# Block-diagonal queries and values of a windowed attention: filled by SBUF-to-SBUF transfers instead of ScalarE and GpSimd, with the block number as innermost axis

## The reference

```python
x = x + _L0_xattn_ref(_layernorm(x, axis=-1), ctx_4096, ctx_4096)   # autocorrelation, top 9 shifts
x = x + _L0_ffn_ref(_layernorm(x, axis=-1), ...)                    # base matrix + 8 experts of rank 16
x = x + _L1_xattn_ref(_layernorm(x, axis=-1), ctx_4096, Wq, bq, ...) # the windowed attention
x = x + _L1_ffn_ref(_layernorm(x, axis=-1), ...)                    # 4 experts of rank 16

def _L1_xattn_ref(x, cond, Wq, bq, Wk, bk, Wv, bv, Wo, bo):
    B, C, T = x.shape                     # 32, 128, 1024
    H, W = (HEADS, WINDOW)                # 8, 16
    hd = C // H                           # 16
    q = _pointwise(Wq, bq, x)
    k = _pointwise(Wk, bk, cond)
    v = _pointwise(Wv, bv, cond)
    ...
    dots = jnp.einsum('bhdt,bhdtw->bhtw', qh, k_win) * scale
    attn = jax.nn.softmax(dots, axis=-1)
    out = jnp.einsum('bhtw,bhdtw->bhdt', attn, v_win)
    out = out.reshape(B, C, T)
    return _pointwise(Wo, bo, out)
```

## Time and profile before

| | |
|---|---|
| Time, median of 3 executions | 1869.83 us (1869.39 to 1873.03) |
| Profiled execution, span | 1871.1 us; this lies inside the spread of the three |
| Busy, share of the span | PE 92%, DVE 84%, ACT 73%, POOL 55% |
| TensorE clock granted | full (1.00) from 400 to 1400 us |
| Transfers | 77.82 MB, mean 42 GB/s |

### The profile page before, as it was taken

One profiled execution on the slowest core, in us unless ns is written; L12 is line 12 of the kernel. 1 busy time (PEld: TensorE's weight loads), 2 busy tenths in 40 slices (PEclk: granted clock), 3 DMA queues, 4 the chain that ended last, 5 costly groups with the idle time before them and its releaser, 6 DMA issues. The chain is left out here.

```text
span 1871.1 us, 48299 instructions
## 1 busy us (share of the span) xinstructions
PE 1712.3 (92%) x19296; PEld 1078.5 (58%) x19296; DVE 1575.8 (84%) x4726; ACT 1372.6 (73%) x2121; POOL 1028.3 (55%) x934
## 2 busy tenths in 40 slices
PE   3689999999999999999999999999999999999875
PEld 1355566666556656556666655666665566565543
DVE  5778898888888888889888888988888888888853
ACT  4277777878777787877777887778787777878753
POOL 1555556556555656655556655555565556566542
PEclk7899999999999999999999999999999999999995
DMA  5111110111010111101011110101110101111000
GB/s 208 34 35 36 35 46 25 47 46 46 24 47 27 44 46 47 47 24 47 24 47 46 47 38 33 46 25 47 46 46 24 47 28 43 46 47 35 2 12 24
DMA packets 20977, 77.82 MB, mean 42 GB/s; under 512 B 2704, under 2 KB 2960, under 8 KB 20240
## 3 DMA queue, kind: packets, MB, share of 16 engines
q1 hardware_dynamic: 20752, 74.72, 11.7%
HBM read 57.94 MB, written 16.78 MB: 40 GB/s over the span
## 5 line engine op out<-in xcount | busy, mean ns | idle before, releaser
L586 PE MATMUL pb<-w_base_h,even_words 128*128 128x512 f16 x1024 | 324.8, 379 | 0.0
L1438 POOL TENSOR_TENSOR p_hl<-sc,p_hl 128x512 f16<-128x512 f32 x128 | 164.2, 1283 | 206.6 <-ACT p_hl L764 206.6
L877 ACT ACTIVATE q_diag<-sc,par 32x512 f32<-32x512 f32 x384 | 269.4, 717 | 8.0
L1483 POOL TENSOR_TENSOR sc<-sc,sc_rec 128x512 f32<-128x512 f32 x128 | 134.4, 1050 | 216.8 <-DVE sc_rec L1245 216.6
L586 PE MATMUL pb<-w_base_l,even_words 128*128 128x512 f16 x512 | 193.9, 379 | 0.0
L473 PE MATMUL pa<-xn_a,tab 128*128 128x512 f32 x384 | 180.5, 606 | 4.6 <-ACT xn_a L764 4.6
L660 PEld LDWEIGHTS pc<-sc_t,v_diag 128*128 128x128 f16 x6144 | 170.2, 97 | 20.6 <-DVE sc_t L1252 6.0
L660 PE MATMUL pc<-sc_t,v_diag 128*128 128x32 f16 x6144 | 173.9, 177 | 5.6 <-DVE sc_t L1252 5.6
L637 PE MATMUL pc<-k_h,q_diag 128*128 128x32 f16 x2048 | 169.1, 177 | 0.0
L638 PE MATMUL pc<-k_l,q_diag 128*128 128x32 f16 x2048 | 168.4, 177 | 0.0
L639 PE MATMUL pc<-k_h,q_diag 128*128 128x32 f16 x2048 | 168.4, 177 | 0.0
(11 more groups left out here) (170 smaller groups left out, 5008.1 us busy)
## 6 DMA issues: line engine op xcount, KB each, us to landing
x_a<-in_x SPq DMA_DIRECT2D x32, 512.0 KB, 3.6
x_res<-in_ctx_in SPq DMA_DIRECT2D x32, 512.0 KB, 4.4
x_res<-in_x SPq DMA_DIRECT2D x32, 512.0 KB, 4.5
out<-rows_c SPq DMA_DIRECT2D x32, 512.0 KB, 2.9
v_diag<-in_base_w SPq DMA_DIRECT2D x4, 1024.0 KB, 10.4
q_diag<-in_ra SPq DMA_DIRECT2D x1, 544.0 KB, 14.1
q_diag<-in_b SPq DMA_DIRECT2D x1, 512.0 KB, 15.8
q_diag<-in_b SPq DMA_DIRECT2D x2, 256.0 KB, 17.0
```

The lines of the kernel that those rows point to most:

```text
L586: mm(pb[:, h, :], rows[:, cols], weights[:, j, h * HALF:(h + 1) * HALF], start=(j == 0 and m == 0), stop=False)
L877: nc.scalar.activation(q_diag[rows, blocks, col:col + QB], source, ACT.Copy, scale=par[rows, a:a + 1]).then_inc(qd_out.sem, 1)
L1438: g_.tensor_tensor(part[:, :, :, LO], sc[:, g % 2, :, :], part[:, :, :, HI], ALU.subtract)\
L1483: g_.tensor_tensor(sc[:, g % 2, :, :], sc[:, g % 2, :, :], sc_rec[:, blocks].unsqueeze(2).to_broadcast([P, GB, KEYS]), ALU.mult)\
```

## The change

Both buffers get the block number as innermost axis: `q_diag` is [rows, 128 columns, 64 blocks] and `v_diag` is [rows, odd/even, 128 columns, 32 blocks]. `q_hl` and `v_t` get the same order, so that what a head contributes is one contiguous run in a row. The copies of ACT and POOL go away. SP issues 8 transfers from `v_t` to `v_diag` (32 rows, two runs of 2 KB a row) and 8 from `q_hl` to `q_diag` (16 rows, a run of 4 KB a row) for each batch. The other four transfers are ordered anew in SP's loop. The first score group now waits for all queries of the batch.

```diff
-        q_diag = sb("q_diag", [P, NBLK, P])
-        v_diag = sb("v_diag", [P, NBLK, 2, P // 2])
+        q_diag = sb("q_diag", [P, P, NBLK])
+        v_diag = sb("v_diag", [P, 2, P, NBLK // 2])
...
+        q_words = q_hl.bitcast(F16).rearrange("p (t n two) -> p n t two", t=QB, two=2)
...
+            def place_values(b, odd):
+                sp.wait_ge(vt_out.sem, vt_out.after(b, odd + 1))
+                if odd == 0:
+                    sp.wait_ge(vdiag_set.sem, 1)
+                    if not first(b):
+                        sp.wait_ge(mm_av.sem, mm_av.after(b - 1))
+                for pair in range(PAIRS):
+                    rows = slice(32 * pair, 32 * pair + 32)
+                    place = v_diag[rows, odd, :, :].rearrange("p (a r d) m -> p a r (d m)", a=2, r=PAIRS)
+                    sp.dma_start(place[:, :, pair, :], v_t[odd][rows, :].rearrange("p (a n) -> p a n", a=2))\
+                        .then_inc(v_placed.sem, 16)
+
+            def place_queries(b):
+                sp.wait_ge(ql_out.sem, ql_out.after(b))
+                sp.wait_ge(qdiag_set.sem, 1)
+                if not first(b):
+                    sp.wait_ge(mm_sc.sem, mm_sc.after(b - 1))
+                for head in range(HEADS):
+                    rows = slice(HD * head, HD * (head + 1))
+                    sp.dma_start(q_diag[rows, rows, :], q_hl[rows, :].rearrange("p (t n) -> p t n", t=QB))\
+                        .then_inc(q_placed.sem, 16)
...
                 if live(1):
                     load_x_res(i - 1)
-                if live(3):
-                    store(i - 3)
+                if live(2):
+                    place_values(i - 2, 0)
+                if live(-1) and not first(i):
+                    load_x(i + 1)
+                if live(2):
+                    place_values(i - 2, 1)
+                    place_queries(i - 2)
                 if live(-1):
                     load_ctx(i + 1)
-                if live(-2):
-                    load_x(i + 2)
+                if live(3):
+                    store(i - 3)
...
-                if g % 2 == 0:
-                    pe.wait_ge(qd_out.sem, qd_out.after(b, (g // 2 + 1) * 2 * (PAIRS - 1)))
-                    pe.wait_ge(qd_pool.sem, qd_pool.after(b, (g // 2 + 1) * 2))
                 if g == 0:
+                    pe.wait_ge(q_placed.sem, q_placed.after(b))
...
-                    mm(place, q_halves[:, blk, :, HI], k_h[:, keys], start=False, stop=False)
-                    mm(place, q_halves[:, blk, :, HI], k_l[:, keys], start=False, stop=False)
-                    last = mm(place, q_halves[:, blk, :, LO], k_h[:, keys], start=False, stop=(i == GB - 1))
+                    mm(place, q_halves[:, :, blk, HI], k_h[:, keys], start=False, stop=False)
+                    mm(place, q_halves[:, :, blk, HI], k_l[:, keys], start=False, stop=False)
+                    last = mm(place, q_halves[:, :, blk, LO], k_h[:, keys], start=False, stop=(i == GB - 1))
...
-                        last = mm(place, v_halves[:, blk, :, v_part], p_halves[:, g % 2, i, :, p_part],
+                        last = mm(place, v_halves[:, blk % 2, :, blk // 2, v_part], p_halves[:, g % 2, i, :, p_part],
...
-                nc.scalar.activation(words(q_hl)[:, :, HI], pb_all, ACT.Identity, bias=bias_att[:, 0:1])\
+                nc.scalar.activation(q_words[:, :, :, HI], pb_all.rearrange("p (n t) -> p n t", t=QB), ACT.Identity, bias=bias_att[:, 0:1])\
                     .then_inc(qh_out.sem, 1)
...
-                v.transpose(v_t[odd], v_pad[:, odd * QB:odd * QB + D]).then_inc(vt_out.sem, 1)
+                v.transpose(v_t[odd].rearrange("p (c m) -> p m c", m=NBLK // 2), v_pad[:, odd * QB:odd * QB + D]).then_inc(vt_out.sem, 1)
...
-                low_half(words(q_hl)[:, :, LO], pb_all, 0, words(q_hl)[:, :, HI], ql_out)
+                low_half(q_words[:, :, :, LO], pb_all.rearrange("p (n t) -> p n t", t=QB), 0, q_words[:, :, :, HI], ql_out)
```

More of the change, by code:

```diff
@@ L378, in build @@
         WEIGHTS_SPLIT = SPLITS + 3
-        base_f32 = v_diag[:, :, :, :].rearrange("p n a c -> p (n a c)")
-        q_flat = q_diag[:, :, :].rearrange("p n c -> p (n c)")
+        base_f32 = v_diag[:, :, :, :].rearrange("p o c m -> p (o c m)")
+        q_flat = q_diag[:, :, :].rearrange("p c n -> p (c n)")
         ra0_f32 = q_flat[:, 0:KT * (E0 + P)]
@@ L843, in b_values @@
                                      bias=bias_att[:, 2:3]).then_inc(vh_out.sem, 1)
-            def b_value_blocks(b, odd, pair):
-                if pair == 0:
-                    act.wait_ge(vt_out.sem, vt_out.after(b, odd + 1))
-                    if odd == 0:
-                        act.wait_ge(vdiag_set.sem, 1)
-                        if not first(b):
-                            act.wait_ge(mm_av.sem, mm_av.after(b - 1))
-                rows = slice(32 * pair, 32 * pair + 32)
-                place = v_diag[rows, :, :, pair * HD:(pair + 1) * HD]\
-                    .rearrange("p (m o) a d -> p o m a d", o=2)[:, odd]
-                copy(place, v_t[odd][rows, :].rearrange("p (m a d) -> p m a d", a=2, d=HD))\
-                    .then_inc(vd_out.sem, 1)
             def b_queries(b):
@@ L862, in b_queries @@
                     act.wait_ge(pl_out.sem, pl_out.after(b - 1))
-                nc.scalar.activation(words(q_hl)[:, :, HI], pb_all, ACT.Identity, bias=bias_att[:, 0:1])\
+                nc.scalar.activation(q_words[:, :, :, HI], pb_all.rearrange("p (n t) -> p n t", t=QB), ACT.Identity, bias=bias_att[:, 0:1])\
                     .then_inc(qh_out.sem, 1)
-            def b_query_blocks(b, pair, a, half):
-                if pair == 0 and a == 0:
-                    act.wait_ge(ql_out.sem, ql_out.after(b))
-                    act.wait_ge(qdiag_set.sem, 1)
-                    if not first(b):
-                        act.wait_ge(mm_sc.sem, mm_sc.after(b - 1, 2 * half + 2))
-                rows = slice(32 * pair, 32 * pair + 32)
-                blocks = slice(half * NBLK // 2, (half + 1) * NBLK // 2)
-                source = q_hl[rows, :].rearrange("p (n t) -> p n t", t=QB)[:, blocks]
-                col = (2 * pair + a) * QB
-                nc.scalar.activation(q_diag[rows, blocks, col:col + QB], source, ACT.Copy,
-                                     scale=par[rows, a:a + 1]).then_inc(qd_out.sem, 1)
             def experts_exp(b, n, source, experts):
@@ L900, in c_high @@
                 if g == 0:
[L901 removed]
+                    act.wait_ge(v_placed.sem, v_placed.after(b))
                 act.wait_ge(p_out.sem, p_out.after(b, g + 1))
```

82 lines of the change are left out of this document (8 added, 74 removed).

## The result

The kernel takes **3474.4 us** (median of 4 runs, 3469.5 to 3478.4) where the kernel before took 1871.4 beside it: a ratio of **1.857** (95% interval 1.854 to 1.860). The 1871.4 is the median of four executions, one of which was a slow one of 2011.5 us that the ratio leaves out. Forecast were 2228 us in a range of 1880 to 2700. The sign was right, the size far off.

A forecast was written before the change was run, and what follows sets the result against it. PE was taken to bound the kernel. Per step, 9.6 weight loads + 2.2 late queries + 0.4 DVE - 1.0 removed copies = 11.2 us, 358 us in all, giving 2228 us as median; range 1880 to 2700.

The forecast's parts named there:

- cheap case: Query transfers on SP: transposed odd values ready at 940.40, eighth issue starts at 945.9, lands 2.9 us later: 1.0 us late.
- the 2.2: Chosen lateness of the query transfers, 2.2 us a step, between 1.0 and 4.1 but nearer the low end.
- What bounds the kernel: PE sets the pace, busy 52.87 of 55.5 us a step; DVE close behind with 48.3 us.
- The 2.6 us of gaps: PE's idle time a step: the most that work taken off ACT and POOL can give back, 83 us in all.
- Weight loads with a wide step: PE's 384 products a batch on both buffers: slot grows from 25 to 50 ns, costing 9.6 us a step.
- the bound of 38.0: Upper bound for PE's weight loads: each slot grows by the f32 load's extra 99 ns, 38.0 us a step.
- free loads: Rival: PE reads wide columns at the old pace, only queries come late; 1871 to 2009 us; chance 0.28.
- dear loads: Rival: PE's wide weight loads cost 38.0 us a step in place of 9.6; 3138 us, above 2470; chance 0.13.
- Queries by transfer: ACT's high part, DVE's low part, eight SP issues and the last landing delay PE's first product 2.2 us a step.
- dear case: Query transfers: all four writes with the wide step take twice as long; 4.1 us late, or 5.7 with slower landing.
- DVE elsewhere: A longer even transpose on DVE pushes the step's second normalisation; 0.4 us a step, bounds 0 and 1.2.
- SP's queue: Value transfers, residual and context loads and the store on SP: nothing is late from the new order.

## Why the prediction was wrong, step by step

The chain of medians, each step one edit, in us a step of the loop (the difference over 32):

| | us | us a step | forecast |
|---|---|---|---|
| no fills at all, against before | -21 | -0.65 | -1.0 |
| all transfers, packed writes, narrow loads | +111 | +3.5 | 1.0 late queries in the cheap case |
| writes in the wide order | +160 | +5.0 | the other 1.2 of the 2.2, and 0.4 on DVE |
| weights 256 and 128 bytes apart | +1352 | +42.2 | +9.6 |
| sum | +1603 | +50.1 | +11.2 |

**What bounds the kernel.** Right: copies beside PE are worth almost nothing (0.65 us a step, forecast 1.0), and work added to PE is paid in full. The 2.6 us of gaps were no reserve: without any fill PE is still idle 33 of 1000 us.

**Weight loads with a wide step: the step that failed.** The prediction saw the term, placed it on the path, and gave a reason against free loads that the steps of 8 and 16 bytes bear out, that 0.2 ns a column asks for several columns an access. Then it took the size from the wrong row: "The f32 load is about twice the f16 load, so between ends far apart I take that ratio for the slot: 25 ns becomes 50 ns". The f32 columns also lie side by side, so that row says nothing on distance. Measured are 120 ns for 192 products and 90 for the other 192: 192 x 95 + 192 x 65 ns = 30.7 us a step, 983 us in all, below the bound of 38.0 and three times the 9.6. The rival "free loads", with 0.28, is out: narrow loads alone bring 1352 us back. The rival "dear loads" was the right one, with 0.13, and the range of 1880 to 2700 ended below that rival's own sum of 3138. That sum was still 336 too low. About 134 us of this are the loads' (42.2 us a step for 38.0), the rest are the late chain and the slow writes. And the loads' 42.2 are made otherwise than that rival has it, since they have a second price that no term had:

**The clock and the neighbours.** Of 42.2 us a step the slots explain 30.7; 11.5 us, 369 in all, are left. Windows of 2 us over one score group of the changed kernel (1398 to 1404) and the f32 products behind it (1404 to 1408):

```profile
1398.00:1400.00 2.00, 1.77 (x15) 1.76 (x16) 0.18 (x2) 2.00 (x1) 0.74 (x2) 1.00 0.65 229
1400.00:1402.00 2.00, 2.00 (x18) 2.00 (x19) 0.00 (x0) 1.98 (x2) 0.00 (x0) 0.65 0.00 0
1402.00:1404.00 2.00, 2.00 (x19) 2.00 (x19) 0.00 (x0) 2.00 (x1) 0.00 (x0) 0.50 0.03 8
1404.00:1406.00 2.00, 2.00 (x6) 1.01 (x6) 1.60 (x3) 1.83 (x2) 0.11 (x1) 0.50 0.00 0
1406.00:1408.00 2.00, 2.00 (x7) 0.97 (x6) 0.61 (x2) 0.63 (x1) 2.00 (x1) 0.64 0.00 0
1408.00:1410.00 2.00, 2.00 (x19) 1.97 (x18) 2.00 (x1) 1.71 (x2) 0.24 (x1) 1.00 0.00 0
```

In the group the granted clock falls from 1.00 (2.4 GHz) to 0.50 (1.2 GHz), while PE is busy all the time with products of 32 columns that wait for their weights. It is so in every step here: at the end of all 128 score groups the clock stands at 0.50; in 104 of them it fell inside the group, in 24 it was low already. In the kernel before it fell inside one of 128. The group itself doesn't care: the score products start 120 ns apart at 1.00 and 121 at 0.50 (medians). Those behind it do, until the clock comes back: L611's products start 216 ns apart at 1.00 and 427 at 0.50, and the four f32 products at 1404.20 take 3.56 us, and 1.96 in the kernel before.

PE's timeline adds up to the whole difference. The profiled execution of the changed kernel is 1360 us longer than that of the kernel with narrow loads. From each start to the next, the products on the two buffers take 971 us more (580 and 391) and all other products 388 us more. PE's idle time is the same, 329 and 327 us (the span less PE's busy time on the two pages). The other products spend 1002 us at the low clock, and 210 with narrow loads; half of the difference is 396 us, an estimate of what the low clock costs them, and it covers the 388. L611 shows it alone: busy 669 us, and 519 with narrow loads as before. That the idle 5.6 us a step ahead of `mid_hl` are not the reason is seen in the kernel with packed writes and wide loads: it lacks most of them (PE 959 of 1000 us busy) and has the same clock of 0.79.

The slowed accesses of others are shown (`v_im` 3132 ns, `xn_a` 4444, both normal with narrow loads), but they lie beside PE: with its idle time unchanged and the other products explained by the clock, nothing of the 11.5 us is left for them in the sum.

**Queries by transfer: right place in one kernel, wrong in the other.** With packed writes PE waits 2.3 us a step for the transfer, as the last paragraph of the prediction foretold (2 us); in the changed kernel it is 0.4. The issues were under-priced, 0.63 us each for 0.50, twelve in a row 7.6 us for 6.0; landing was over-priced, 2.3 us for 2.9. Of the 3.5 us, 109 us between the two profiled executions, 66 are idle time of PE and 43 are longer products. 35 of these are L498's on `xn_a`, of which about a quarter run at the low clock (start to start 854 ns for 429).
With the writes in the wide order the "dear case" was a doubling and the measured factor 3.5 for the queries: ACT's high part 1421 to 4946 ns, DVE's low part 1383 to 4767, against 28% for the nearest row, which I had leaned to. Only the transposes were near a doubling (1.23 to 1.97 and 2.14 us). The "4.1 us late" of that case became 5.6, and for another instruction: not the product that reads `q_diag`, but L700, whose input DVE makes after the low part. The prediction had asked who waits for SP and not who waits for DVE.

**DVE elsewhere, SP's queue.** The 0.4 us on DVE is inside the 5.0 and was not measured apart. Nothing was late from the order on SP, as forecast: no other transfer is among the long waits.

**The profile after, as foretold.** Right: groups longer, ACT, DVE and POOL with smaller shares. Wrong: starts 90 and 120 ns apart, over the 65 that the prediction named as the sign of a term too small; PE's share is 91%, not up, since the wait for `mid_hl` grew with it; a wait of 0.4 us a step for the transfer, not 2; ACT is 4 us a step shorter, not 15, since its high part takes 3.5 us more and `v_im` and others are slowed.

## What to carry to other kernels

A layout is paid for by its most frequent reader: here 384 weight loads a batch read what 24 copies wrote, so columns that a load takes must stay side by side, however much nicer the fill becomes. Price a stride from rows with strides only, and if there is none, put the upper bound into the forecast; steps of 128 and 256 bytes were the worst here, and one word of padding gave back half of the loss. When an instruction gets slow on an engine, follow that engine's order to the next result that PE wants, and ask what the slow stretch does to the clock of the products after it.

## What the runs showed of the hardware

- Weight loads of 128 columns with a 32-column product each: 25 ns a product at 4 bytes from column to column, 33 at 8, about 60 at 16 to 64, 132, 252 and 260, 90 at 128, 120 at 256. The 120 and the 90 ns are the same at either clock. The Trainium skill (TensorE: Matmul & The Clock Gate, section on weight-path perf modes) lets the fast load take strided columns up to 1,024 elements and names no price; by that rule alone these loads would all be alike, and they are not: the slot more than doubles from 4 to 16 bytes.
- PE that was busy without a gap in a score group of the changed kernel was granted half the clock (0.50) by the end of each of the 128 groups, and L611's 512-column products behind it took 479 ns in the mean and not 379.
- While loads with a step of 256 bytes run, accesses of others slow down, in the mean over the launch ACT from 1019 to 3132 ns, DVE from 1214 to 4444, and POOL's product of probabilities from 1050 to 1527. With steps of 128, 252 and 260 bytes they don't (1.00 to 1.02 times).
- f16 writes of 1024 elements: 1114 ns packed, 1429 at 4 bytes apart, 4946 at 256 bytes.
- A transfer within SBUF costs its queue 0.6 us with runs of 2 KB and more, and 1.0 us with 1024 runs of 64 bytes.
